# Second feed-forward: the rank-2 product of gate*up with a2, from one TensorE product a step to a VectorE sum a block

## The chip, the cores and the metric

One NeuronCore of a Trainium2 chip runs the whole kernel. The metric is the device time of one execution in microseconds (us), the median of several runs; lower is better. Engines: TensorE (PE; PEld is its weight load), VectorE (DVE), ScalarE (ACT), GpSimd (POOL), SyncE (SP, which issues DMAs).

## The reference, cut to what matters

```python
x = layernorm(x + attn(x, w_gate, w_up, w_down))            # first feed-forward, sparse, 2752 wide
def qlora(x, wq, A, B):
    w = jnp.tile(wq, (1, 4))                                # wq holds a quarter of the input columns
    return x @ w.T + (x @ A.T @ B.T) * 0.5                  # A, B of rank 2
gate = silu(qlora(x, w1q, a1, b1)); up = qlora(x, w3q, a3, b3)
x = layernorm(x + qlora(gate * up, w2q, a2, b2))            # second feed-forward
```

x has 2048 tokens of 1024 values, all in float32; the hidden width is 2752. Because w2 is tiled four times, the product of gate*up (called h) with it needs only the sum of h over its four quarters, 688 wide. The rank-2 product h @ a2.T needs all 2752 values of h.

## The kernel before

Tokens go in four blocks of 512 (NB, TB). The first feed-forward fills most of the time; the change concerns the second, which starts near 1690 us and is written in functions named with _2. Every float32 operand of a product is split into a high part (type fp32r) and a low part, the remainder; ScalarE makes the high part, GpSimd the low one (`low`, line 465), and TensorE adds three products (`three`, lines 1277 to 1279).

A block has 22 steps (STEPS), m = 4c + q. c is one of six chunks of the quarter's 688 rows (five of 128, the last of 112 for a pair of quarters), q the quarter; the last chunk has two steps. In a step TensorE makes gate and up of 128 hidden rows by 512 tokens: six 512-column products and one low-rank product (line 1448) for each, in PSUM banks 2(m%2) and 2(m%2)+1. ScalarE takes silu of the gate into sg (line 831), VectorE multiplies with up into h2 (line 1197) and adds h2 to fold (lines 1205, 1208) for q over 0. ScalarE splits h2 into h2h (line 817), GpSimd makes h2l (line 570), and TensorE multiplies both with a2s, the split a2 of that step, into bank 4 (`low_h`, lines 1420 and 1423), two steps behind. When a chunk's fold is complete ScalarE makes hqh (line 822) and GpSimd hql (line 576).

After the steps, `down_2` multiplies hqh and hql with w2 for four token tiles (t) and two halves (n), and adds the low-rank part t2s x b2s (line 1478). Between tiles the next block's x1 is transposed (line 1401), copied (line 807), multiplied with a1 and a3 (line 1410) and summed over quarters by VectorE (`fold_x`, lines 1166 to 1172). VectorE's `low_rank_h` takes bank 4 into t2s (lines 1223 to 1226).

The order of work is written by hand: each engine runs its instructions in program order and waits on semaphores. What matters here:
- TensorE's gate of step m waits until ScalarE has read the bank of step m-2, its up until VectorE has (h_done).
- A chunk's first step waits for the low parts (w13l) of its four weight pieces. The pieces of chunk c+1 are loaded when chunk c-1 has been used (pe_used), made high by ScalarE in steps q of chunk c, and low by GpSimd in the same steps, in its queue before that step's other work.
- In steps 1 to 4 VectorE also takes the mean and variance of the previous block's y (lines 1067 to 1072); GpSimd's `inv_std` (line 507) waits for it in its queue at step 5.
- The last c of down_2's first half waits for all six hql.

Of the kernel before, what the change touches and what calls it, by code (L numbers as in the profile page):

```python
# [26 lines left out]
P = 128  # L27
# [37 lines left out]
NW2, NW13 = 2 * CQ, 4 * CQ  # L65
USED2 = USED0 + USEDB * (NB - 1) + ND
# [50 lines left out]
def program(nc, xT, xtok, wg, wu, wd, w13, w2, a13, a2, b1, b3, b2, out):  # L117
    x1 = nc.dram_tensor("x1", (NB, P, NT, H), F32, kind="Internal").ap()
    with ExitStack() as ctx:
        def sem(name):  # L120
            return ctx.enter_context(nc.semaphore(name))
# [83 lines left out]
        a2s = put("a2s", [P, STEPS, 2 * R], F32R)  # L205
# [3 lines left out]
        t2s = put("t2s", [P, TB], F32R)  # L209
        assert over["at"] <= at["hTh"]  # L210
# [18 lines left out]
        h2 = put("h2", [P, 2, TB], F32)  # L229
        h2h = put("h2h", [P, 2, TB], F32R)  # L230
        h2l = put("h2l", [P, 2, TB], F32R)
# [9 lines left out]
        def down_done_with(name, h):  # L241
# [4 lines left out]
        hql = put("hql", [P, CQ, TB], F32R)  # L246
        assert over["at"] <= at["junkd"]

# [18 lines left out]
        small_in, b_zero, b_in, b_ready, a_ready, keep_ready = (  # L267
            sem("small_in"), sem("b_zero"), sem("b_in"), sem("b_ready"), sem("a_ready"), sem("keep_ready"))
        l_fold = sem("l_fold")
        x1t_done, x1t_ready, t1_done, l_ready = sem("x1t_done"), sem("x1t_ready"), sem("t1_done"), sem("l_ready")  # L270
        gg_done, uu_done, s_done, h_done, f_done = (
            sem("gg_done"), sem("uu_done"), sem("s_done"), sem("h_done"), sem("f_done"))
        hh_done, hl_done, t2_done, t2_ready = sem("hh_done"), sem("hl_done"), sem("t2_done"), sem("t2_ready")
# [179 lines left out]
        def _(pool):  # L453
# [80 lines left out]
            for d in range(ND):  # L534
                sl = slice((d % 4) * 512, (d % 4 + 1) * 512)
                rows = rows_in(NC - 1 - d // 2)
                low(LAST_D + d, wh[0:rows, sl], wl[0:rows, sl], w_in_place[0:rows, sl])
                if d == 4:

                    pool.wait_ge(t_done, NC * NB)  # L540
                    nc.gpsimd.memset(keep[:], 1.0).then_inc(pool_s, 1)
                    pool.wait_ge(pool_s, 3)
                    nc.gpsimd.affine_select(out=keep[:, 0:1], in_=keep[:, 0:1], compare_op=ALU.is_ge, fill=0.0,
                                            base=R - 1, pattern=[[0, 1]], channel_multiplier=-1).then_inc(keep_ready, 1)
                    nc.gpsimd.affine_select(out=keep[:, 1:2], in_=keep[:, 1:2], compare_op=ALU.is_ge, fill=0.0,
                                            base=-R, pattern=[[0, 1]], channel_multiplier=1).then_inc(keep_ready, 1)
                    nc.gpsimd.memset(t2s[0:LR, :].bitcast(F32), 0.0).then_inc(keep_ready, 1)
                if d == 19:
# [16 lines left out]
            def steps_2(b, last):  # L565

                def low_h(m):
                    rows = place(m)[2]
                    pool.wait_ge(hh_done, STEPS * b + m + 1)
                    nc.gpsimd.tensor_tensor(h2l[0:rows, m % 2, :], h2[0:rows, m % 2, :],  # L570
                                            h2h[0:rows, m % 2, :].bitcast(F32), ALU.subtract).then_inc(hl_done, 1)
# [17 lines left out]
                low_h(STEPS - 1)  # L589
# [17 lines left out]
        def _(act):  # L607
# [202 lines left out]
            def steps_2(b, before):  # L810

                def high_h(m):
                    rows = place(m)[2]
                    act.wait_ge(h_done, STEPS * b + m + 1)
                    if m >= 2:
                        act.wait_ge(t2_done, STEPS * b + m - 1)
                    nc.scalar.copy(h2h[0:rows, m % 2, :], h2[0:rows, m % 2, :]).then_inc(hh_done, 1)  # L817

                def high_q(c):
                    rows = rows_of(c)  # L820
                    act.wait_ge(f_done, CQ * b + c + 1)
                    nc.scalar.copy(hqh[0:rows, c, :], fold[0:rows, :]).then_inc(qh_done, 1)

                for m in range(STEPS):
                    c, q, rows = place(m)
                    if c < CQ - 1:
                        high_13(b, c + 1, q)
                    act.wait_ge(gg_done, STEPS * b + m + 1)
# [3 lines left out]
                    if m:  # L832
                        high_h(m - 1)
                    if q == 0 and c:
                        high_q(c - 1)
# [8 lines left out]
                high_h(STEPS - 1)  # L844
# [28 lines left out]
        def _(dve):  # L873
# [261 lines left out]
            with dve.Fori(1, NB) as b:  # L1135
# [12 lines left out]
            step(V.tensor_copy(a2s[:, :, 0:R], a2raw[:, :, :]))  # L1148
            st.done()
            V.tensor_tensor(a2s[:, :, R:2 * R], a2raw[:, :, :], a2s[:, :, 0:R].bitcast(F32), ALU.subtract)\  # L1150
                .then_inc(a_ready, 1)
# [37 lines left out]
            def steps_2(b):  # L1189
                for m in range(STEPS):  # L1190
# [9 lines left out]
                    last = q == steps_of(c) - 1  # L1200
                    ins = None
                    if q == 1:
                        if c:
                            dve.wait_ge(ql_done, CQ * b + c)
                        ins = V.tensor_tensor(fold[0:rows, :], h2[0:rows, 0, :], h2[0:rows, 1, :], ALU.add)
                    elif q > 1:
                        st.done()
                        ins = V.tensor_tensor(fold[0:rows, :], fold[0:rows, :], h2[0:rows, m % 2, :], ALU.add)
                    if last:
                        ins.then_inc(f_done, 1)  # L1210
                        dve.wait_ge(f_done, CQ * b + c + 1)
                    elif ins is not None:
                        step(ins)
# [5 lines left out]
            def low_rank_h(b):  # L1219

                n = 2 * R
                dve.wait_ge(t2_done, STEPS * (b + 1))
                step(V.tensor_copy(t2s[0:n, :], banks[4][0:n, :]))
                step(V.tensor_copy(t2s[64:64 + n, :], banks[4][0:n, :]))
                st.done()
                V.tensor_tensor(t2s[32:32 + n, :], banks[4][0:n, :], t2s[0:n, :].bitcast(F32), ALU.subtract)\
                    .then_inc(t2_ready, 1)
# [44 lines left out]
        def _(pe):  # L1272
# [141 lines left out]
            def low_h(b, m, frees):  # L1414

                c, q, rows = place(m)
                pe.wait_ge(hl_done, STEPS * b + m + 1)
                pe.sem_inc(passed_pe, 1)
                w = a2s[0:rows, m, :]
                i1 = nc.tensor.matmul(banks[4][0:2 * R, :], w, h2h[0:rows, m % 2, :], start=m == 0, stop=False)  # L1420
                if frees:
                    i1.then_inc(pe_used, 4)
                nc.tensor.matmul(banks[4][0:2 * R, :], w, h2l[0:rows, m % 2, :], start=False,
                                 stop=m == STEPS - 1).then_inc(t2_done, 1)

            def steps_2(b):
# [3 lines left out]
                for m in range(STEPS):  # L1430
# [8 lines left out]
                    for i, (low_x, done) in enumerate(((lg, gg_done), (lu, uu_done))):  # L1439
# [4 lines left out]
                        for k in range(KQ):  # L1444
                            s, mm = (c % 2) * 4 + 2 * i + k, slice(q * rows, (q + 1) * rows)
                            three(dst, w13h[:, s, mm], w13l[:, s, mm], xsh[:, k, :], xsl[:, k, :], k == 0, False)
                        mm = slice(c * Q4 * P + q * rows, c * Q4 * P + (q + 1) * rows)
                        nc.tensor.matmul(dst, b13[0:LR, mm], low_x[0:LR, :], start=False, stop=True).then_inc(done, 1)  # L1448
                    if m >= 2:
                        low_h(b, m - 2, q == steps_of(c) - 1)  # L1450
                low_h(b, STEPS - 2, False)

            def down_2(b, t, between=None):
# [8 lines left out]
                for n in range(2):  # L1462
                    w = slice(n * 512, (n + 1) * 512)
                    for c in range(CQ):
                        rows = rows_of(c)
                        if t == n == 0 and c == CQ - 1:
                            low_h(b, STEPS - 1, False)
# [19 lines left out]
            pe.wait_ge(a_ready, 1)  # L1487
# [78 lines left out]
```

## Time and profile before

| | |
|---|---|
| median of 3 runs | 2202.78 us (2202.04 to 2204.5) |
| profiled execution, span from first to last instruction | 2205.2 us (no other time of this execution is given) |
| TensorE busy | 2058.3 us, 93% |
| VectorE busy | 1110.3 us, 50% |
| GpSimd busy | 1053.4 us, 48% |
| ScalarE busy | 782.8 us, 35% |

The profile records one execution. Busy times of TensorE overlap in part, as matmuls are pipelined. A row of the timeline has the start in us, the duration in us, engine, line, operation, output and inputs, and in brackets the idle time before it and what released it.

### The profile page before, as it was taken

What the parts mean: (1) busy time and instruction counts of PE and PEld (TensorE: products, weight loads), DVE (VectorE), ACT (ScalarE), POOL (GpSimd) and SP (SyncE); (2) the same over time, 40 slices, a digit from 0 to 9 for tenths busy, and PEclk for the clock granted to TensorE, in tenths of its full rate; (3) what the DMA queues carried; (4) which work ended last, traced back from release to release, by engine and by line L of the source; (5) the groups of instructions that cost most, each with busy time, mean ns of one, the idle gap of its engine ahead of it and who ended that gap; (6) DMA issues with size and microseconds to landing.
All of it is one profiled execution on the core that took longest, in us unless ns stands there. A gap on an engine that the chain in (4) does not pass through costs nothing.

```text
span 2205.2 us, 32819 instructions
## 1 busy us (share of the span) xinstructions
PE 2058.3 (93%) x11008; PEld 1834.4 (83%) x11008; DVE 1110.3 (50%) x1794; ACT 782.8 (35%) x1280; POOL 1053.4 (48%) x744
## 2 busy tenths in 40 slices
PE   8998949999799899979989999799997999999998
PEld 8997939978699898869989888798786777777776
DVE  0145863368665234886533479654005444453543
ACT  3345323354133234612333363132233515334151
POOL 6444734435344443444454345343474827447281
PEclk9998969999899998989999999898999999999999
DMA  4332403322343332233433223244332412314030
GB/s 128 96 92 63 127 15 91 88 82 96 111 124 114 92 91 72 96 121 90 121 111 92 73 96 130 78 122 131 121 108 78 143 57 86 133 38 151 32 138 39
DMA packets 90356, 213.47 MB, mean 97 GB/s; under 512 B 10360, under 2 KB 12408, under 8 KB 89188
## 3 DMA queue, kind: packets, MB, share of 16 engines
q1 hardware_dynamic: 85616, 194.97, 28.8%
q10 hardware_dynamic: 4608, 16.78, 2.0%
q8 instruction: 78, 1.28, 0.2%
q14 instruction: 54, 0.44, 0.1%
HBM read 194.93 MB, written 16.78 MB: 96 GB/s over the span
## 4 chain that ended last, share of the span: by engine, by line
PE 71%; issue 11%; POOL 8%; DVE 5%; ACT 3%; DMA 2%; SPq 0%; POOLq 0%; ACTq 0%; DVEq 0%
PE bank L1277 22%; PE bank L1278 22%; PE bank L1279 22%; POOL wl L465 3%; POOL h2l L570 2%; ACT junka L672 2%; POOL w13l L465 2%; PE bank L1410 1%; DVE v L1122 1%; PE bank L1448 1%; DMA w_in_place<-in_wu 1%; PE bank L1309 1%; DMA w_in_place<-in_wd 1%; DVE scr L969 1%; ACT wh L613 1%
## 5 line engine op out<-in xcount | busy, mean ns | idle before, releaser
L465 POOL TENSOR_TENSOR wl<-w_in_place,wh 128x688 fp32r<-128x688 f32 (+1 forms) x432 | 680.1, 1576 | 826.5 <-ACT wh L613 806.1
L1277 PE MATMUL bank<-wh,xTh 128*128 128x344 f32 x2048 | 666.9, 326 | 79.4 <-POOL wl L465 49.5
L1279 PE MATMUL bank<-wh,xTl 128*128 128x344 f32 x2048 | 662.5, 323 | 0.0
L1278 PE MATMUL bank<-wl,xTh 128*128 128x344 f32 x2048 | 661.6, 323 | 0.0
L613 ACT CAST wh<-w_in_place 128x688 fp32r<-128x688 f32 (+1 forms) x432 | 305.3, 707 | 929.1 <-DMA w_in_place<-in_wu 352.8
L1277 PEld LDWEIGHTS bank<-wh,xTh 128*128 128x128 f32 x2048 | 392.0, 191 | 83.2 <-issue 68.7
L1278 PEld LDWEIGHTS bank<-wl,xTh 128*128 128x128 f32 x2048 | 392.4, 192 | 0.0
L1279 PEld LDWEIGHTS bank<-wh,xTl 128*128 128x128 f32 x2048 | 391.6, 191 | 0.0
L1277 PE MATMUL bank<-wh,hTh 128*128 128x512 f32 (+1 forms) x704 | 284.6, 404 | 11.8 <-ACT v L642 6.6
L1278 PE MATMUL bank<-wl,hTh 128*128 128x512 f32 (+1 forms) x704 | 283.1, 402 | 0.0
L1279 PE MATMUL bank<-wh,hTl 128*128 128x512 f32 (+1 forms) x704 | 282.6, 401 | 0.0
L465 POOL TENSOR_TENSOR w13l<-w_in_place,w13h 128x512 fp32r<-128x512 f32 (+1 forms) x96 | 124.6, 1303 | 187.1 <-ACT w13h L613 186.9
L1277 PEld LDWEIGHTS bank<-wh,hTh 128*128 128x128 f32 (+1 forms) x704 | 137.3, 195 | 46.9 <-issue 13.6
L905 DVE TENSOR_SCALAR sgn<-v x96 | 69.5, 724 | 204.4 <-ACT v L642 204.4
L672 ACT ACTIVATE junka<-v,negt 128x1376 int8<-128x1376 f32 x96 | 138.3, 1441 | 76.0 <-DVE negt L915 76.0
L1279 PEld LDWEIGHTS bank<-wh,hTl 128*128 128x128 f32 (+1 forms) x704 | 137.5, 195 | 29.8
L1278 PEld LDWEIGHTS bank<-wl,hTh 128*128 128x128 f32 (+1 forms) x704 | 137.5, 195 | 28.8
L1277 PE MATMUL bank<-xsh,w13h 128*128 128x512 f32 (+1 forms) x352 | 140.6, 399 | 9.0 <-DVEq L1187 5.5
L921 DVE TENSOR_SCALAR_CACHE_REDUCE junkd<-v,tc 128x2752 int8<-128x2752 f32 x48 | 147.6, 3076 | 0.9
L1197 DVE TENSOR_TENSOR h<-bank,sg 128x512 f32<-128x512 f32 (+1 forms) x88 | 60.8, 691 | 171.6 <-PE bank L1448 153.7
L1113 DVE TENSOR_TENSOR hTl<-bank,hTh 128x512 fp32r<-128x512 f32 x88 | 55.6, 683 | 180.6 <-ACT hTh L690 180.4
L570 POOL TENSOR_TENSOR h2l<-h,h2h 128x512 fp32r<-128x512 f32 (+1 forms) x88 | 120.2, 1366 | 44.2 <-ACT h2h L817 44.2
(128 smaller groups left out, 2535.9 us busy)
## 6 DMA issues: line engine op xcount, KB each, us to landing
w_in_place<-in_wg SPq DMA_DIRECT2D x128, 344.0 KB, 2.9
w_in_place<-in_wu SPq DMA_DIRECT2D x128, 344.0 KB, 2.9
w_in_place<-in_wd SPq DMA_DIRECT2D x168, 256.0 KB, 2.6
w_in_place<-in_w SPq DMA_DIRECT2D x90, 256.0 KB, 3.7
x_in_place<-in_xT SPq DMA_DIRECT2D x32, 256.0 KB, 3.4
y<-in_xtok SPq DMA_DIRECT2D x4, 2048.0 KB, 8.7
x<-y ACTq DMA_DIRECT2D x16, 512.0 KB, 3.5
xa<-x SPq DMA_DIRECT2D x16, 512.0 KB, 4.5
```

Of the source, the lines that this page charges most:

```text
L465: nc.gpsimd.tensor_tensor(lo, landed, hi.bitcast(F32), ALU.subtract).then_inc(done, 1)
L570: nc.gpsimd.tensor_tensor(h2l[0:rows, m % 2, :], h2[0:rows, m % 2, :], h2h[0:rows, m % 2, :].bitcast(F32), ALU.subtract).then_inc(hl_done, 1)
L613: nc.scalar.copy(hi, piece).then_inc(hi_done, 1)
L672: ins = nc.scalar.activation(junka[:, :], v[:, t, h * (I // 2):(h + 1) * (I // 2)], ACT.Sign, bias=negt[:, t:t + 1], accum_out=ssum[:, t - ...
L905: step(V.tensor_scalar(sgn[:, t, bass.ds((2 * jj + q) * CW, CW)], s, 0.0, 2.0, ALU.is_ge, ALU.mult))
L921: step(V.tensor_scalar(junkd[:, :], v[:, t, :], tc[:, 0, t:t + 1], None, ALU.is_lt, ALU.add, accum_out=tc[:, 1, t:t + 1]))
L969: step(V.scalar_tensor_tensor(out=scr[:], in0=v[:, t, c * Q:(c + 1) * Q], scalar=hc[:, 0, t:t + 1], in1=v[:, t, c * Q:(c + 1) * Q], op0=AL ...
L1113: V.tensor_tensor(hTl[0:rows, c, :], banks[4 * (j % 2) + m][0:rows, :], hTh[0:rows, c, :].bitcast(F32), ALU.subtract).then_inc(t_lo, 1)
L1197: V.tensor_tensor(h2[0:rows, m % 2, :], banks[2 * (m % 2) + 1][0:rows, :], sg[0:rows, m % 2, :], ALU.mult).then_inc(h_done, 1)
L1277: nc.tensor.matmul(dst, ah, bh, start=start, stop=False)
L1278: nc.tensor.matmul(dst, ah, bl, start=False, stop=False)
L1279: return nc.tensor.matmul(dst, al, bh, start=False, stop=stop)
```

## The change

The product of h with a2 is no longer made on TensorE in each step. VectorE keeps acc, two sums of 128 x 512 for each block, and adds h2 times a column of a2 to each in every step. After the last step it splits acc into acch and accl, and four products with sel (ones in one column for each rank row) add them over partitions, into bank 4, within down_2 of tile 0 (n = 1, before c = 3). The sum over quarters moves from VectorE to GpSimd (`fold_h`). h2h and h2l are gone, h2 has four buffers instead of two, and the weights' buffers are released at the last product of a chunk's up. t2s is filled by two operations instead of three, behind which fold_x of the next block's first tile stands in VectorE's queue. hqh is made at q = 1 of the next chunk instead of q = 0.

```diff
 VectorE, steps_2
-                    if m >= 2:
-                        dve.wait_ge(hl_done, STEPS * b + m - 1)
+                    if m >= H2N:
+                        dve.wait_ge(folded, FOLDS * b + folds_by(m - H2N))
...
-                        ins = V.tensor_tensor(fold[0:rows, :], h2[0:rows, 0, :], h2[0:rows, 1, :], ALU.add)
...
+                    for r in range(R):
+                        w, total = a2raw[0:rows, m, r:r + 1], acc[0:rows, r, :]
+                        if m == 0:
+                            step(V.tensor_scalar(total, hm, w, None, ALU.mult))
+                        else:
+                            step(V.scalar_tensor_tensor(out=total, in0=hm, scalar=w, in1=total, op0=ALU.mult, op1=ALU.add))
 VectorE, low_rank_h
+                step(V.tensor_copy(acch[:, :, :], acc[:, :, :]))
+                st.done()
+                V.tensor_tensor(accl[:, :, :], acc[:, :, :], acch[:, :, :].bitcast(F32), ALU.subtract).then_inc(acc_ready, 1)
+                dve.wait_ge(t2_done, b + 1)
+                step(V.tensor_copy(t2s[0:LR, :], banks[4][0:LR, :]))
+                st.done()
+                V.tensor_tensor(t2s[32:64, :], banks[4][32:64, :], t2s[32:64, :].bitcast(F32), ALU.subtract)\
 GpSimd, steps_2
+                def fold_h(m):
+                    c, q, rows = place(m)
+                    pool.wait_ge(h_done, STEPS * b + m + 1)
+                    if q > 1:
+                        pool.wait_ge(folded, FOLDS * b + m - c - 1)
+                    elif c:
+                        pool.wait_ge(ql_done, CQ * b + c)
+                    before = h2[0:rows, (m - 1) % H2N, :] if q == 1 else fold[0:rows, :]
+                    nc.gpsimd.tensor_tensor(fold[0:rows, :], before, h2[0:rows, m % H2N, :], ALU.add).then_inc(folded, 1)
...
-                    if m:
-                        low_h(m - 1)
-                    if q == 0 and c:
+                    if q == 1 and c:
                         low_q(c - 1)
+                    if m and q != 1:
+                        fold_h(m - 1)
                     if m == 5:
                         inv_std(NB + b - 1)
 TensorE
-            def low_h(b, m, frees):
-                pe.wait_ge(hl_done, STEPS * b + m + 1)
...
+            def low_h(b):
+                pe.wait_ge(acc_ready, b + 1)
+                for r in range(R):
+                    nc.tensor.matmul(banks[4][0:LR, :], sel[:, r, :], acch[:, r, :], start=r == 0, stop=False)
+                    ins = nc.tensor.matmul(banks[4][0:LR, :], sel[:, r, :], accl[:, r, :], start=False, stop=r == R - 1)
+                ins.then_inc(t2_done, 1)
```

## Rows read from the trace of the kernel before

**Rows 1.** The page's first part: busy us, share of the span, instructions.
```profile
PE 2058.3 (93%) x11008; PEld 1834.4 (83%) x11008; DVE 1110.3 (50%) x1794; ACT 782.8 (35%) x1280; POOL 1053.4 (48%) x744
```

**Rows 2.** Busy time by stretch: PE, PEld, DVE, ACT, POOL, granted clock, DMA.
```profile
1818.47:1901.40 82.93, 81.58 (x350) 61.01 (x351) 39.29 (x54) 40.31 (x73) 59.40 (x47) 1.00 0.35 120
```

**Rows 3.** Timeline of TensorE, the first matmuls of two steps.
```profile
1828.69 0.40 PE L1277 MATMUL bank<-xsh,w13h 128*128 128x512 f32 x1
...
1832.39 0.40 PE L1277 MATMUL bank<-xsh,w13h 128*128 128x512 f32 x1
```

**Rows 4.** Timeline of VectorE in steps 1 and 7 of the second block.
```profile
1825.20 0.69 DVE L1197 TENSOR_TENSOR h<-bank,sg 128x512 f32<-128x512 f32 x1 [2.41 <-PE bank L1448]
1825.93 0.69 DVE L1205 TENSOR_TENSOR fold<-h 128x512 f32<-128x512 f32 x1
1826.54 1.28 DVE L1067 BATCH_NORM_STATS2 stats<-y 128x6 f32<-128x512 f32 x2
1827.97 0.21 DVE L1069 BATCH_NORM_AGGREGATE mv<-stats 128x2 f32<-128x12 f32 x1 [0.15 <-DVE stats L1067]
...
1847.74 1.78 DVE L1208 TENSOR_TENSOR fold<-fold,h 128x512 f32<-128x512 f32 x1
```

**Rows 5.** Timeline of GpSimd in the same block.
```profile
1826.03 1.75 POOL L465 TENSOR_TENSOR w13l<-w_in_place,w13h 128x512 fp32r<-128x512 f32 x1
...
1842.52 1.01 POOL L507 TENSOR_TENSOR rstd<-ve,mhalf 128x4 f32<-128x4 f32 x1
...
1847.70 1.27 POOL L570 TENSOR_TENSOR h2l<-h,h2h 128x512 fp32r<-128x512 f32 x1
...
1867.85 1.29 POOL L570 TENSOR_TENSOR h2l<-h,h2h 128x512 fp32r<-128x512 f32 x1
1869.10 1.28 POOL L576 TENSOR_TENSOR hql<-fold,hqh 128x512 fp32r<-128x512 f32 x1
```

**Rows 6.** Two lines with durations min/median/max in ns; one group with its mean.
```profile
L1085 DVE SCALAR_TENSOR_TENSOR v<-v,tc x96: 565/577/2074, 590.6 to 1513.1; 128x344 f32<-128x344 f32 x96
...
L969 DVE SCALAR_TENSOR_TENSOR scr<-v,hc x32: 1650/1654/2707, 229.4 to 1369.5; 128x1376 f32<-128x1376 f32 x32
...
L1184 DVE TENSOR_SCALAR lg<-th,keep 4x512 fp32r<-4x512 f32 x6 | 2.9, 476 | 0.2
```

**Rows 7.** Timeline of VectorE and GpSimd near 290 us, merged rows.
```profile
289.16 5.55 DVE L1122 SCALAR_TENSOR_TENSOR v<-v,tc,w 128x344 f32<-128x344 f32 x4
...
289.70 2.77 POOL L465 TENSOR_TENSOR xTl<-x_in_place,xTh 128x512 fp32r<-128x512 f32 x2 [6.94 <-ACT xTh L628]
```

**Rows 8.** Timeline of ScalarE and TensorE: refill of chunk 2, start of step 8.
```profile
1835.08 0.62 ACT L613 CAST w13h<-w_in_place 128x512 fp32r<-128x512 f32 x1 [3.47 <-DMA w_in_place<-in_w]
...
1848.13 0.47 PE L1277 MATMUL bank<-xsh,w13h 128*128 128x512 f32 x1 [0.78 <-POOL w13l L465]
```

**Rows 9.** Timeline of TensorE after an idle time, and the stretch behind it.
```profile
1599.67 0.79 PE L1277 MATMUL bank<-wh,hTh 128*128 128x512 f32 x1 [3.26 <-POOL wl L465]
...
1600.00:1606.00 6.00, 6.00 (x15) 4.65 (x15) 0.00 (x0) 1.24 (x2) 2.33 (x3) 0.51 0.34 133
```

**Rows 10.** Timelines of TensorE and VectorE at the end of the steps.
```profile
1899.52 0.39 PE L1448 MATMUL bank<-lu,b 96*112 96x512 f32 x1
...
1900.95 0.39 PE L1420 MATMUL bank<-h2h,a2s 112*4 112x512 f32 x1 [0.58 <-POOL h2l L570]
...
1905.72 0.40 PE L1420 MATMUL bank<-h2h,a2s 112*4 112x512 f32 x1
...
1899.94 0.69 DVE L1197 TENSOR_TENSOR h<-bank,sg 112x512 f32<-112x512 f32 x1 [3.00 <-PE bank L1448]
```

**Rows 11.** Timeline of VectorE in the down matmuls of tile 0 and 1.
```profile
1906.39 0.68 DVE L1223 CAST t2s<-bank 4x512 fp32r<-4x512 f32 x1 [5.03 <-PE bank L1423]
...
1908.53 1.98 DVE L1166 TENSOR_REDUCE xf<-x1T 128x256 f32<-128x1024 f32 x1
...
1917.87 1.10 DVE L1170 CAST xsh<-xf 128x256 fp32r<-128x256 f32 x1
```

More of the change, by code:

```diff
@@ L65 @@
 NW2, NW13 = 2 * CQ, 4 * CQ
+H2N = 4
+FOLDS = STEPS - CQ
 USED2 = USED0 + USEDB * (NB - 1) + ND
@@ L78, in steps_of, with folds_to, folds_by @@
     return Q4 if c < CQ - 1 else Q4 // 2
+def folds_to(c):
+    return (Q4 - 1) * (c + 1) if c < CQ - 1 else FOLDS
+def folds_by(m):
+    c, q, _ = place(m)
+    done = m + 1 if q == 0 else m
+    return done - place(done)[0]
 def place(m):
@@ L209, in program @@
         t2s = put("t2s", [P, TB], F32R)
+        sel = put("sel", [P, R, LR], F32R)
         assert over["at"] <= at["hTh"]
@@ L228, in program @@
         sg = put("sg", [P, 2, TB], F32)
-        h2 = put("h2", [P, 2, TB], F32)
-        h2h = put("h2h", [P, 2, TB], F32R)
-        h2l = put("h2l", [P, 2, TB], F32R)
+        h2 = put("h2", [P, H2N, TB], F32)
         fold = put("fold", [P, TB], F32)
@@ L246, in program @@
         hql = put("hql", [P, CQ, TB], F32R)
+        acch = put("acch", [P, R, TB], F32R)
+        accl = put("accl", [P, R, TB], F32R)
         assert over["at"] <= at["junkd"]
+        acc = sb("acc", [P, R, TB], F32, 4, offset=at["scr"])
         banks = [bank(f"bank{i}") for i in range(8)]
@@ L547, in _ @@
                     nc.gpsimd.memset(t2s[0:LR, :].bitcast(F32), 0.0).then_inc(keep_ready, 1)
+                    nc.gpsimd.memset(sel[:, :, :].bitcast(F32), 0.0).then_inc(pool_s, 1)
+                    pool.wait_ge(pool_s, 4)
+                    for r in range(R):
+                        nc.gpsimd.memset(sel[:, r, :].bitcast(F32).rearrange("p (g k) -> p g k", g=3)[:, :, r:r + 1],
+                                         1.0).then_inc(sel_ready, 1)
                 if d == 19:
@@ L827, in steps_2 @@
                         high_13(b, c + 1, q)
+                    if q == 1 and c:
+                        high_q(c - 1)
                     act.wait_ge(gg_done, STEPS * b + m + 1)
@@ L1147, in _ @@
             dve.wait_ge(small_in, 16 * 2)
[L1148 to L1151, printed above, removed]
             dve.wait_ge(b_ready, 2)
@@ L1193, in steps_2 @@
                     dve.wait_ge(s_done, STEPS * b + m + 1)
-                    if m >= 2:
-                        dve.wait_ge(hl_done, STEPS * b + m - 1)
+                    if m >= H2N:
+                        dve.wait_ge(folded, FOLDS * b + folds_by(m - H2N))
                     st.done()
-                    V.tensor_tensor(h2[0:rows, m % 2, :], banks[2 * (m % 2) + 1][0:rows, :], sg[0:rows, m % 2, :],
-                                    ALU.mult).then_inc(h_done, 1)
+                    hm = h2[0:rows, m % H2N, :]
+                    V.tensor_tensor(hm, banks[2 * (m % 2) + 1][0:rows, :], sg[0:rows, m % 2, :], ALU.mult).then_inc(h_done, 1)
                     dve.wait_ge(h_done, STEPS * b + m + 1)
[L1200 to L1204, printed above, removed]
-                        ins = V.tensor_tensor(fold[0:rows, :], h2[0:rows, 0, :], h2[0:rows, 1, :], ALU.add)
[L1206 to L1213, printed above, removed]
+                    for r in range(R):
[4 more added lines that the diff above has]
+                            step(V.scalar_tensor_tensor(out=total, in0=hm, scalar=w, in1=total, op0=ALU.mult, op1=ALU.add))
                     if 1 <= m <= NT:
@@ L1412, in low_rank @@
                 ins.then_inc(t1_done, 1)
-            def low_h(b, m, frees):
-                c, q, rows = place(m)
-                pe.wait_ge(hl_done, STEPS * b + m + 1)
+            def low_h(b):
+                pe.wait_ge(acc_ready, b + 1)
                 pe.sem_inc(passed_pe, 1)
[L1419 to L1424, printed above, removed]
+                for r in range(R):
+                    nc.tensor.matmul(banks[4][0:LR, :], sel[:, r, :], acch[:, r, :], start=r == 0, stop=False)
+                    ins = nc.tensor.matmul(banks[4][0:LR, :], sel[:, r, :], accl[:, r, :], start=False, stop=r == R - 1)
+                ins.then_inc(t2_done, 1)
             def steps_2(b):
@@ L1445, in steps_2 @@
                             s, mm = (c % 2) * 4 + 2 * i + k, slice(q * rows, (q + 1) * rows)
-                            three(dst, w13h[:, s, mm], w13l[:, s, mm], xsh[:, k, :], xsl[:, k, :], k == 0, False)
+                            ins = three(dst, w13h[:, s, mm], w13l[:, s, mm], xsh[:, k, :], xsl[:, k, :], k == 0, False)
+                        if i == 1 and q == steps_of(c) - 1:
+                            ins.then_inc(pe_used, 4)
                         mm = slice(c * Q4 * P + q * rows, c * Q4 * P + (q + 1) * rows)
                         nc.tensor.matmul(dst, b13[0:LR, mm], low_x[0:LR, :], start=False, stop=True).then_inc(done, 1)
-                    if m >= 2:
-                        low_h(b, m - 2, q == steps_of(c) - 1)
-                low_h(b, STEPS - 2, False)
             def down_2(b, t, between=None):
@@ L1465, in down_2 @@
                         rows = rows_of(c)
+                        if t == 0 and n == 1 and c == 3:
+                            low_h(b)
                         if t == n == 0 and c == CQ - 1:
-                            low_h(b, STEPS - 1, False)
                             pe.wait_ge(ql_done, CQ * (b + 1))
@@ L1486, in _ @@
             pe.wait_ge(b_ready, 4)
[L1487 removed]
+            pe.wait_ge(sel_ready, R)
             pe.wait_ge(keep_ready, 5)
```

35 lines of the change are left out of this document (7 added, 28 removed).

## The prediction

> **What bounds the kernel now.** I read the page's engine shares first. TensorE is busy 93% of the span; an average that says nothing of the second feed-forward [rows 1]. So I cut that out by stretches: each of its four blocks has 22 steps and then its down matmuls, and the steps of the second block take 82.93 us with 350 matmuls [rows 2]. Then the TensorE timeline: a step of sixteen 512-column matmuls runs from 1828.69 to 1832.39, 3.70 us, or 0.231 a matmul; the recorded 0.40 overlaps [rows 3]. 350 x 0.231 is 80.9 of the 82.93; two waits, 0.78 for w13l and 0.58 for h2l, make most of the rest [rows 8, 10]. So the steps are bound by TensorE today, with almost nothing under it to spare.
>
> But the work around it is near that bound. GpSimd is busy 59.4 and VectorE 39.3 of the 82.93 [rows 2], and the timelines of both show that they exclude each other. GpSimd's h2l starts at 1847.70, VectorE's fold at 1847.74 and takes 1.78 instead of 0.69: it is held 1.09. The other way round, the fold of 1825.93 makes w13l take 1.75 instead of 1.29 [rows 4, 5]. h = bank x sg, with one input in PSUM, takes 0.69 beside anything [rows 10]. GpSimd operations follow each other at 1.25 when nothing is in the way [rows 5]. With a fold of 0.69 between two of them, the fold of 1825.93 ends at 1826.62 and w13l at 1827.78, so one operation takes 1.16 after its release; the held fold ends 0.55 after h2l, not 0.69. The two overlap by 0.14, and one GpSimd operation plus one fold cost about 1.70, of which 1.01 is GpSimd's.
>
> **The change, part by part (block time T from 1818.47, us).**
>
> *TensorE.* Each block loses 22 x 2 matmuls and gains 4: 40 x 0.231 = 9.2, 37.0 over four blocks, if TensorE stays the bound. A step becomes 14 x 0.231 = 3.23.
>
> *VectorE.* One fold in 16 of 22 steps goes; two accumulations a step come. The trace has no 512-wide scalar_tensor_tensor with two SBUF inputs and a column scalar, but it has 344 wide at 0.577 and 1376 wide at 1.654 (the medians) [rows 6]: 1.04 ns an element, 0.75 for 512. Bounds: the 0.69 of a fold, and 0.75 plus a held 1.09. The first step's two tensor_scalar are 0.48, by the 4x512 form [rows 6].
>
> *GpSimd.* 22 h2l go and 16 folds come, 48 full or half operations become 42. All of them read SBUF.
>
> *The shared access.* Two accumulations in a row do not keep GpSimd out. In the first phase four such instructions (0.57 each) took 5.55 between 289.16 and 294.71, with GpSimd's xTl in between [rows 7]: they alternate, 2.28 of work and 3.27 of waiting. So in a steady step with two GpSimd operations (w13l and a fold or hql) the cycle is 2 x (1.01 + 0.75), 3.5 to 3.6 with the gaps, above TensorE's 3.23 and just below today's 3.70. This is the middle of the sum. Bounds: 3.23 (never in the way) and 2 x 1.25 + 1.5 = 4.0 (nothing overlaps).
> The Trainium skill says under "SBUF — State Buffer", Who interferes with whom, that a VectorE instruction with two SBUF inputs contends with a GpSimd instruction that reads SBUF and that the loser waits for the whole instruction. That speaks against this change. Taken literally with the 1.29 of the rows it makes a pair 2.04, a step 4.1 and four such steps 16.3 where the rows' overlap gives 14.3; I go by the rows, which overlap.
>
> *Steps 0 to 7.* VectorE also does the previous block's statistics in steps 1 to 4: bn_stats from 1826.54 to bn_aggr's end 1828.18, 1.64 [rows 4]. Such a step costs it 0.73 (h) + 1.5 + 1.0 (a GpSimd fold wedged in, released by the same h) + 1.67 (the statistics and a gap) = 4.9 against a 3.23 step. h(1) can start at T 6.7, as now (1825.20 less 1818.47 is 6.73) [rows 4]. Then h(2) 11.6, h(3) 16.5, h(4) 21.6, and h(5) 25.7 (no fold wedged in, plus ve). TensorE reuses a bank after two steps: up of step 6 (due at 21.0) waits for h(4) until 22.35, 1.35; up of step 7 then waits 0.85 for h(5) and ends at 28.0. GpSimd's queue is w13l(2,1), hql, then inv_std (1.01 [rows 5]), which waits for ve at 25.7; queued behind it are w13l(2,2), the fold of h(5) and w13l(2,3), for which step 8's matmuls wait. 26.7 + three operations of 1.25 + three accumulations in their way (0.5 each; 1.75 against 1.29 is 0.46 for a fold) = 32.0. Today step 8 starts at 1848.13, T 29.7 [rows 8]. TensorE idles 28.0 to 32.0.
> The refill is no later than now: its loads wait for the last matmuls of a chunk, and w13h of the first piece starts at 1835.08, T 16.6 [rows 8].
>
> *The clock.* After an idle of 3.26 TensorE ran 15 matmuls 0.43 apart, at a granted clock of 0.50, the 1.2 GHz level, in 1600 to 1606 [rows 9]. A 4.0 idle I take to do the same: 15 x 0.20 = 3.0 lost. Ends: 0 and 3.0.
>
> *Steps 8 to 21.* The first chunk of four takes TensorE 12.9 + 3.0 = 15.9 and the two other engines 14.3 (8 GpSimd operations of 1.01, 8 accumulations of 0.75, gaps): 15.9. The next takes 14.3 less 0.9, what the two engines can use of their lead: 13.4. The chunk after it has half-size pieces and takes TensorE's 12.9, the last two steps 6.5. Together 48.7: the stretch ends at 80.7 (82.93 now). Ends: 29.7 + 14 x 3.23 = 74.9, and 36 + 51 = 87.
>
> *Down stretch.* Today h(21) starts 0.42 after the last up matmul (1899.52, 1899.94), and TensorE gets to the last c of the down matmuls at 1905.72 without a wait [rows 10]. Afterwards it gets there after eight transposes and 15 matmuls, 3.46; the transposes are 1905.72 - 3.46 less 1901.41 (1900.95 + 2 x 0.231), 0.85, together 4.3 after the steps; the chain it needs is 0.2 + h 0.69 + accumulation 0.75 + fold 1.15 on GpSimd + hqh 0.6 + cast of acc + hql 1.15 + gaps 0.3. The cast (0.48 for 512 wide, so 0.5 to 1.0 for 1024; I take 0.8) stands in GpSimd's way, since a 256 wide one of 1917.87 was held to 1.10 itself [rows 6, 11]: 5.6. Wait 1.3 (0 to 2.5). Two matmuls more, 0.46. The t2s chain (two operations of 0.68 [rows 11] after 0.43) takes 1.8 and ten matmuls 2.3 lie before its use: hidden, 0.4 to spare. fold_x(t=0) moves behind it, some 5 us later. The low-rank matmuls of tile 1 want its x1T 5.0 after tile 0 ends (0.85 + 18 x 0.231); fold_x's reduce takes 2.0 [rows 11], two copies and gaps as much again: hidden, 1.0 to spare.
> The setup (a2s gone, memsets of sel on GpSimd in the last down phase) I cost at nothing: twelve matmuls a piece, 2.8, lie over a w piece of 1.25. Without that cover it is 1 us once.
>
> **Sum.** Per block 80.7 + 1.3 + 0.46 against 82.93 is -0.5; four blocks about -2: 2203.2 by the profiled execution, whose span of 2205.2 lies 2.4 above the median of the runs, so 2201 as a median. The matmuls saved are spent on two engines that shut each other out.
>
> **Rivals.**
> *TensorE stays near the bound (faster).* If VectorE does both accumulations before GpSimd gets in, steps 1 to 4 cost 3.9 each, step 8 starts at about 29.3, no idle is long enough for the clock and the middle chunks take 13.6: 29.3 + 27.2 + 12.9 + 6.5 + 1.8 = 77.7, -5.3 a block, 2182. For it: a fold that starts within 0.14 of the end of h2l isn't held. Against it: [rows 7], where they alternate.
> *The statistics and inv_std hold the queue (slower).* If in steps 1 to 4 both accumulations wait for a whole GpSimd operation (w13l and a fold), VectorE loses 1.0 more a step, inv_std comes 4 later, step 8 at 36 and TensorE idles 8 in a row. +4 a block: 16 - 2, 2217. It decides from 1.6 a block on, which takes the whole 4.4 above now. For it: folds held for 1.09 today. Against: GpSimd has one operation only in steps 0 and 1, and waits for h itself in 2 and 3.
> *It doesn't do what it says (no collision, full gain)*: -37 + 4 x 1.8 = -30, 2173; against it are the held pairs of [rows 4, 5], and I give it a small part of the faster case.
>
> **How the numbers follow.** 0.2%, 4.4 us, is about what a measurement of this kernel can tell from no change. Forecast case 0.45, its own range 2195 to 2207: 0.10 faster, 0.28 same, 0.07 slower. Faster rivals 0.33, slower rival 0.22. Together 0.43, 0.28, 0.29. The range runs from the middle of the fast rival to half way into the slow one, 2183 to 2213.
>
> **What would show it.** Right: 308 matmuls in a step stretch of 80 to 82; accumulations with a minimum of 0.75 and a mean over 1.1; folds on GpSimd over 1.5; TensorE waiting for w13l at step 8 by some 4 us in each block, a granted clock of 0.5 behind it; h(4) and h(5) late. Wrong: w13l waits under 1 us and a mean accumulation under 0.9 (the fast rival), or h late throughout and step 8 beyond T 34 (the slow one). If no wait for ql appears in the down stretch, that term was mis-sized.

## The result, and the profile after

| | median of runs | ratio to the runs of before, 95% |
|---|---|---|
| before | 2202.78 us (7 runs) | |
| changed | 2214.55 us (7 runs) | 1.0048 (1.0032 to 1.0063) |
| changed, second series | 2219.1 us (10 runs; before beside it 2206.39) | 1.0055 (1.0035 to 1.0076) |

The change makes the kernel 0.5% slower, 10.6 to 12 us, where 2201 had been forecast. The profiled execution has a span of 2209.3, only 4.1 above that of before; its run is the shortest of the seven (2211.05 with what lies around the span), while the span of before alone is above the median of its runs. So these two profiles show only part of the loss; the other part is seen in the further profiles below. Medians of different series are not to be subtracted: a series is compared by its ratio to the runs of before beside it.

The page's first part of the changed kernel, the same columns as [rows 1]: TensorE is busy 25 us less and VectorE 149 more.
```profile
PE 2032.8 (92%) x10848; PEld 1825.4 (83%) x10848; DVE 1259.6 (57%) x1908; ACT 738.9 (33%) x1192; POOL 1063.6 (48%) x723
```
The four step stretches by window, columns as [rows 2]; the second answers to it. 308 matmuls instead of 350, but 80.99 instead of 82.93, and in three of the four stretches a granted clock under 1.00 (before, 0.97 in the first stretch and 1.00 in the others):
```profile
1686.10:1771.05 84.95, 76.95 (x308) 60.74 (x309) 69.14 (x77) 29.42 (x50) 58.08 (x40) 0.94 0.33 117
1819.71:1900.70 80.99, 72.78 (x308) 57.27 (x309) 71.55 (x79) 29.42 (x50) 59.39 (x40) 1.00 0.35 123
1949.21:2031.87 82.66, 75.17 (x309) 59.11 (x310) 73.01 (x79) 29.64 (x50) 59.63 (x40) 0.96 0.35 120
2080.39:2163.75 83.36, 75.86 (x308) 59.61 (x309) 70.00 (x79) 29.43 (x50) 58.16 (x40) 0.96 0.27 94
```
Before, these stretches took 84.99, 82.93, 82.98 and 82.69. The saving is 0.0, 1.9, 0.3 and -0.7, 1.6 in all.

VectorE in steps 3 to 5 of the second block (it answers to [rows 4]; two accumulations are merged in a row), block time T counted from 1819.71:
```profile
1836.21 0.69 DVE L1209 TENSOR_TENSOR h<-bank,sg 128x512 f32<-128x512 f32 x1
1836.94 2.72 DVE L1216 SCALAR_TENSOR_TENSOR acc<-h,a2raw,acc 128x512 f32<-128x512 f32 x2
1839.59 1.27 DVE L1082 BATCH_NORM_STATS2 stats<-y 128x6 f32<-128x512 f32 x2
1841.01 0.21 DVE L1084 BATCH_NORM_AGGREGATE mv<-stats 128x2 f32<-128x12 f32 x1 [0.15 <-DVE stats L1082]
1841.38 0.69 DVE L1209 TENSOR_TENSOR h<-bank,sg 128x512 f32<-128x512 f32 x1 [0.16 <-DVE mv L1084]
1842.11 1.42 DVE L1216 SCALAR_TENSOR_TENSOR acc<-h,a2raw,acc 128x512 f32<-128x512 f32 x2
...
1845.39 0.69 DVE L1209 TENSOR_TENSOR h<-bank,sg 128x512 f32<-128x512 f32 x1
```
Two accumulations take 1.42 when GpSimd is idle (it waits for ve then) and 2.72 when it is not. GpSimd beside them (answers to [rows 5]):
```profile
1837.37 1.74 POOL L596 TENSOR_TENSOR fold<-fold,h 128x512 f32<-128x512 f32 x1
1839.08 1.74 POOL L480 TENSOR_TENSOR w13l<-w_in_place,w13h 128x512 fp32r<-128x512 f32 x1
1840.78 1.26 POOL L601 TENSOR_TENSOR hql<-fold,hqh 128x512 fp32r<-128x512 f32 x1
1845.37 1.02 POOL L522 TENSOR_TENSOR rstd<-ve,mhalf 128x4 f32<-128x4 f32 x1 [3.33 <-DVE ve L1087]
1846.36 1.66 POOL L480 TENSOR_TENSOR w13l<-w_in_place,w13h 128x512 fp32r<-128x512 f32 x1
1847.98 1.71 POOL L596 TENSOR_TENSOR fold<-h 128x512 f32<-128x512 f32 x1
1849.65 1.72 POOL L480 TENSOR_TENSOR w13l<-w_in_place,w13h 128x512 fp32r<-128x512 f32 x1
```
And TensorE's waits in that block, with what ended each: up of step 6, up of step 7, gate of steps 8, 12 and 16, and the down matmuls' wait for the last hql (answers to [rows 8, 10]):
```profile
1842.22 0.47 PE L1282 MATMUL bank<-xsh,w13h 128*128 128x512 f32 x1 [1.30 <-DVE h L1209]
...
1846.23 0.47 PE L1282 MATMUL bank<-xsh,w13h 128*128 128x512 f32 x1 [0.55 <-DVE h L1209]
...
1851.76 0.47 PE L1282 MATMUL bank<-xsh,w13h 128*128 128x512 f32 x1 [3.68 <-POOL w13l L480]
...
1866.43 0.47 PE L1282 MATMUL bank<-xsh,w13h 128*128 128x512 f32 x1 [1.29 <-POOL w13l L480]
...
1880.97 0.47 PE L1282 MATMUL bank<-xsh,w13h 128*128 128x512 f32 x1 [1.39 <-POOL w13l L480]
...
1905.56 0.47 PE L1282 MATMUL bank<-w2h,hqh 112*128 112x512 f32 x1 [0.39 <-POOL hql L601]
```
The stretches behind the wait at step 8 in the second and third block (answers to [rows 9]). Waits of 3.68 and 3.66 stand before them; behind the second the clock is at the 1.2 GHz level for part of the stretch, behind the first it is not:
```profile
1851.80:1857.00 5.20, 5.20 (x23) 4.19 (x24) 5.13 (x6) 1.06 (x2) 4.68 (x3) 1.00 0.21 78
...
1981.20:1987.20 6.00, 5.95 (x16) 4.72 (x17) 4.67 (x5) 1.82 (x3) 4.72 (x3) 0.57 0.13 49
```
What such a drop costs is seen in GpSimd's queue. Its first w13l for step 16, in the second block (no drop) and in the third (drop), waits for w13h:
```profile
1869.54 1.30 POOL L480 TENSOR_TENSOR w13l<-w_in_place,w13h 128x512 fp32r<-128x512 f32 x1 [1.80 <-ACT w13h L638]
...
2000.70 1.30 POOL L480 TENSOR_TENSOR w13l<-w_in_place,w13h 128x512 fp32r<-128x512 f32 x1 [3.11 <-ACT w13h L638]
```
In block time that is T 49.8 and 51.5. The loads of these pieces wait until TensorE has used the chunk of steps 8 to 11, and are issued at T 45.4 and 47.8. So a slower TensorE also sends the two other engines off later, and the third block is 1.7 longer.

The groups of the changed kernel's second feed-forward (behind the bar: busy us, mean ns of one): accumulations 1258 ns where 0.75 us is their own price, w13l and fold 1578 and 1631 ns instead of 1.29 us.
```profile
L1216 DVE SCALAR_TENSOR_TENSOR acc<-h,a2raw,acc 128x512 f32<-128x512 f32 x152 | 185.2, 1258 | 2.7
L480 POOL TENSOR_TENSOR w13l<-w_in_place,w13h 128x512 fp32r<-128x512 f32 x75 | 118.2, 1578 | 165.0 <-ACT w13h L638 165.0
L596 POOL TENSOR_TENSOR fold<-fold,h 128x512 f32<-128x512 f32 x40 | 65.2, 1631 | 18.1 <-DVE h L1209 18.1
```
Something else stands before the second feed-forward begins, near 1590. GpSimd waits 6.22 for TensorE before the memset of braw (the buffer of the low-rank weights), and TensorE then waits 4.60 and 1.64 for wl behind it (first GpSimd, then TensorE):
```profile
1586.86 3.27 POOL L570 MEMSET braw<- 96x3808 f32 x1 [6.22 <-PE bank L1284]
...
1591.40 0.80 PE L1282 MATMUL bank<-wh,hTh 128*128 128x512 f32 x1 [4.60 <-POOL wl L480]
...
1601.54 0.50 PE L1282 MATMUL bank<-wh,hTh 128*128 128x512 f32 x1 [1.64 <-POOL wl L480]
```
In the kernel before the memset waits for nothing, and one wait of 3.26 stands there [rows 9]:
```profile
1584.79 3.28 POOL L550 MEMSET braw<- 96x3808 f32 x1
```

### The profile page after: what moved, and what is told of

Read it like the earlier page. It is cut to its first block, busy times and chain, and to the rows that moved or that the text cites. A ratio compares the mean times of both kernels' runs of the same rounds, so it can differ in the third digit from the quotient of the medians.

```text
span 2209.3 us, 32337 instructions
## 1 busy us (share of the span) xinstructions
PE 2032.8 (92%) x10848; PEld 1825.4 (83%) x10848; DVE 1259.6 (57%) x1908; ACT 738.9 (33%) x1192; POOL 1063.6 (48%) x723
## 4 chain that ended last, share of the span: by engine, by line
PE 60%; issue 15%; POOL 9%; DVE 9%; ACT 3%; DMA 2%; POOLq 0%; DVEq 0%; SPq 0%; ACTq 0%
PE bank L1282 19%; PE bank L1284 19%; PE bank L1283 19%; POOL wl L480 5%; DVE acc L1216 3%; ACT junka L697 2%; POOL fold L596 2%; PE bank L1415 1%; DVE h L1209 1%; DVE v L1137 1%; DMA w_in_place<-in_wd 1%; POOL w13l L480 1%; POOL hql L601 1%; DVE stats L1082 1%; PE bank L1314 1%
## 5 line engine op out<-in xcount | busy, mean ns | idle before, releaser
L480 POOL TENSOR_TENSOR w13l<-w_in_place,w13h 128x512 fp32r<-128x512 f32 (+1 forms) x96 | 137.9, 1440 | 185.3 <-ACT w13h L638 185.3
L1216 DVE SCALAR_TENSOR_TENSOR acc<-h,a2raw,acc 128x512 f32<-128x512 f32 (+1 forms) x168 | 202.3, 1243 | 2.9
L1283 PE MATMUL bank<-xsl,w13h 128*128 128x512 f32 (+1 forms) x352 | 142.4, 405 | 0.0
```

What stands on the lines that cost most here:

```text
L480: nc.gpsimd.tensor_tensor(lo, landed, hi.bitcast(F32), ALU.subtract).then_inc(done, 1)
L1216: step(V.scalar_tensor_tensor(out=total, in0=hm, scalar=w, in1=total, op0=ALU.mult, op1=ALU.add))
L1283: nc.tensor.matmul(dst, ah, bl, start=False, stop=False)
```

## The experiments

Each profile is cut at the first step: what lies before it (A) and from there to the end (B). B is the second feed-forward; A repeats to a few us only, and B of the changed kernel to 3. Each other row is one profile.

| kernel | A | B | median | ratio to before, 95% |
|---|---|---|---|---|
| before, two profiles | 1686.1, 1682.5 | 519.1, 520.0 | 2202.78 | |
| changed, two profiles | 1686.1, 1697.5 | 523.2, 526.3 | 2214.55 | 1.0048 |
| acc in PSUM | 1688.7 | 484.6 | 2174.42 | 0.9868 (0.9849 to 0.9887) |
| one accumulation | 1696.0 | 492.9 | 2189.0 | 0.9927 (0.9909 to 0.9946) |
| none | 1691.8 | 483.5 | 2176.37 | 0.9873 (0.9852 to 0.9895) |
| statistics spread | 1690.9 | 519.4 | 2212.77 | 1.0047 (1.0029 to 1.0066) |
| layout as before | 1684.6 | 522.2 | 2208.63 | 1.0020 (1.0003 to 1.0036) |
| TensorE kept busy | 1691.8 | 514.8 | 2208.23 | 1.0007 (0.9992 to 1.0022) |
| inv_std later | 1689.2 | 522.6 | 2211.96 | 1.0044 (1.0027 to 1.0062) |
| PSUM, spread, layout | 1686.0 | 483.6 | 2171.31 | 0.985 (0.9828 to 0.9872) |
| PSUM, layout, inv_std later | 1687.1 | 482.2 | 2165.79 | 0.9824 (0.9798 to 0.9851) |

**Accumulators in PSUM.**
```diff
-                        w, total = a2raw[0:rows, m, r:r + 1], acc[0:rows, r, :]
+                        w, total = a2raw[0:rows, m, r:r + 1], banks[(4, 7)[r]][0:rows, :]
```
and acch, accl are taken from the banks, one r at a time; the next block's low-rank products into bank 7 wait for that.

> The changed kernel with acc kept in PSUM (banks 4 and 7) instead of SBUF, so an accumulation has one SBUF input; it is split into acch and accl from there. Theory A (the two engines shut each other out over SBUF): an accumulation takes about 0.75 us without being held (1.24 mean now), the folds and w13l on GpSimd go back to 1.3, a statistics step costs VectorE 3.95 instead of 4.9, TensorE waits for w13l at step 8 by 1.7 instead of 3.6, later chunks not at all; steps 74 to 75 us a block, the whole about 2175 to 2182. Theory B (VectorE simply has too much work in steps 1 to 4, whoever else reads SBUF): the waits at step 8 stay over 3 us and the time within 5 of the changed kernel, 2208 or more.

Measured 2174.42, 1.8% or 40 us under the changed kernel by the ratios, and 0.6 under the range of theory A. The number of instructions on VectorE and GpSimd is the same but for two more splits a block. The groups (same columns as above):
```profile
L1216 DVE SCALAR_TENSOR_TENSOR bank<-h,a2raw,bank 128x512 f32<-128x512 f32 x152 | 107.5, 753 | 2.7
L480 POOL TENSOR_TENSOR w13l<-w_in_place,w13h 128x512 fp32r<-128x512 f32 x75 | 96.6, 1291 | 183.0 <-ACT w13h L638 183.0
L596 POOL TENSOR_TENSOR fold<-fold,h 128x512 f32<-128x512 f32 x40 | 51.7, 1292 | 13.7 <-DVE h L1209 13.7
```
All three are back at their own price, the step stretch of the second block is 73.4, and TensorE waits for w13l only 1.24 at step 8. So it is not VectorE's amount of work that did the harm but where the accumulator lies. The edit moves both its reading and its writing out of SBUF. That the writing is harmless is seen in the changed kernel itself: h (bank x sg, one SBUF input, written to SBUF) takes 691 ns on average there and never over 694, while the accumulations beside it were held, and 692 here. What is left is the second SBUF input. The Trainium skill has the rule in "SBUF — State Buffer", Who interferes with whom: a VectorE instruction with at most one SBUF input, outside the two-port modes, does not contend with GpSimd. The trace agrees, 753 against 1258 ns.

**One accumulation a step, and none.**
```diff
-                    for r in range(R):
+                    for r in range(R if m == 0 else 1):      # none: else 0
```
Both kernels leave out part of the low-rank sum; they serve to measure its cost.

> The changed kernel with one accumulation a step instead of two (the second rank row gets the first step alone: part of the low-rank sum is left out). Theory A: a step then has 2 x 1.01 + 0.75 of shared access, 2.8, below TensorE's 3.23, so the waits of steps 12 and 16 vanish and that of step 8 shrinks to under 1.5: 2182 to 2190. Theory B: the statistics steps cost VectorE 3.2 to 4.2, the wait at step 8 shrinks likewise, but later chunks, where VectorE has room, should not change.

> The changed kernel with no accumulation after the first step (nearly all of the low-rank sum is left out). It measures the whole cost of VectorE's part: with TensorE's 40 matmuls a block gone and nothing in the way, both theories expect steps of 71 to 72 us a block and a down stretch 0.5 to 1 longer, 2168 to 2175. If it stays above 2190, something else of the change costs (fold on GpSimd, the order of the queues).

2189.0 is as A expected; 2176.37 is 1.4 above its range, as the steps took 71.9 to 73.9 a block instead of 71 to 72, and the down stretches 1.4 to 2.4 more than before instead of 0.5 to 1. With one, B is 492.9; with none 483.5, and with both in PSUM 484.6: in PSUM the accumulations cost 1 us, in SBUF the first costs 9 and the second another 30 to 33. The wait of step 12 went with one accumulation, but the expectation failed for the others: step 16 still waited 0.65 to 1.65, and step 8 waited 1.6 to 2.0, not under 1.5.

**The statistics spread out.** Steps 1, 3, 5, 7; inv_std and bias in step 9, and ScalarE's normalisation two steps later (not shown).
```diff
-                    if 1 <= m <= NT:
-                        norm_sums(NB + b - 1, [m - 1])
+                    if m in (1, 3, 5, 7):
+                        norm_sums(NB + b - 1, [m // 2])
```


> The changed kernel with the previous block's statistics in steps 1, 3, 5, 7 instead of 1 to 4, inv_std and the bias in step 9 and the normalisation two steps later. Theory A and B both expect h(4) and h(5) in time and no long wait at step 8, and with it no drop of the clock there. A expects the saturated chunks to remain (steps 12 and 16 wait 1.3 to 2 for w13l, and now step 8 about as much): a gain of 2 to 3 a block, 2203 to 2207. B expects all waits gone: 2185 or less.

2212.77, a miss for both theories: the ratio is that of the changed kernel, though B of its one profile, 519.4, is 4 to 7 shorter. The wait at step 8 fell to 1.8 and came back at step 12 (second block, TensorE):
```profile
1851.52 0.47 PE L1282 MATMUL bank<-xsh,w13h 128*128 128x512 f32 x1 [1.86 <-POOL w13l L480]
...
1861.45 0.47 PE L1282 MATMUL bank<-xsh,w13h 128*128 128x512 f32 x1 [1.50 <-DVE h L1209]
...
1870.79 0.47 PE L1282 MATMUL bank<-xsh,w13h 128*128 128x512 f32 x1 [4.25 <-POOL w13l L480]
```
**inv_std later in GpSimd's queue.** In step 7, behind the last w13l of the chunk.
```diff
+                    if m == 7:
+                        inv_std(NB + b - 1)
                     if q == 1 and c:
                         low_q(c - 1)
...
-                    if m == 5:
-                        inv_std(NB + b - 1)
```


> The changed kernel with inv_std moved in GpSimd's queue from step 5 to step 7, behind the last w13l of that chunk. Theory E (at step 8 it is the place of inv_std, waiting for VectorE's statistics, that holds w13l): w13l(2,2) no longer waits 3.3 for ve plus 1.0 for the operation; what is left is h(5), at T 25.7, its fold and w13l(2,3), some 29.5: the wait of 3.6 at step 8 falls to about 1.5, too short for the clock, the waits for h stay; 2 to 3.5 a block, 2202 to 2208. If only the shared access sets it, the wait stays above 3.

The wait at step 8 fell to 1.3 to 1.6 as expected, but the time stayed: 2211.96 instead of 2202 to 2208. What it gave up came back: up of step 7 waited 1.5 instead of 0.5, and step 12 waited 3.5 instead of 1.3:
```profile
1853.01 0.47 PE L1282 MATMUL bank<-xsh,w13h 128*128 128x512 f32 x1 [1.60 <-POOL w13l L480]
...
1869.63 0.77 PE L1282 MATMUL bank<-xsh,w13h 128*128 128x512 f32 x1 [3.49 <-POOL w13l L480]
```
Both moves say the same. In the second block step 12 starts at T 46.7 in the changed kernel, 47.2 with the statistics spread and 47.6 with inv_std later: the two engines together owe about the same amount by step 12, and the order only chooses where TensorE waits for it.

**TensorE kept busy through the wait.**
```diff
+                    if m == 8:
+                        for k in range(12):
+                            nc.tensor.matmul(banks[4][0:LR, :], sel[:, 0, :], xsh[:, 0, :], start=True, stop=True)
```


> The changed kernel with twelve extra products (2.8 us, sel times xsh into bank 4, result unused) before TensorE's wait for w13l at step 8 in each block. They fit in the 3.6 wait. Theory D (the idle time also costs by the lower clock behind it): no stretch at a granted clock of 0.5 behind step 8, 1.0 to 1.7 us less a block where it dropped, 2 to 6 less in all. If the clock costs nothing beside the wait, the time is that of the changed kernel within 2.

2208.23, with 48 useless products more; beside it the changed kernel took 2219.1 (1.0007 against 1.0055). B is 514.8 against 523.2 and 526.3: 8 to 11, where I had expected 2 to 6. Behind step 8 of the second block, first the changed kernel's second profile, then this one:
```profile
1864.90:1870.90 6.00, 5.94 (x15) 4.72 (x16) 4.70 (x5) 1.79 (x3) 4.74 (x3) 0.55 0.16 62
```
```profile
1855.50:1861.50 6.00, 5.97 (x26) 4.95 (x27) 5.89 (x7) 1.79 (x3) 4.74 (x3) 1.00 0.20 72
```
No step stretch of this kernel shows a lowered clock after the first 7 us of B. In the two profiles of the changed kernel the clock records of the steps behind those first 7 us hold 20 and 31 us at the 1.2 GHz level; at half speed that is up to 10 and 15 of matmul time, against a gain of 8.4 and 11.5. By this kernel the drops of the clock make up the whole of the second feed-forward's loss: without them B is 4 to 5 below that of before, though the engines are as much in each other's way as in the changed kernel.

**The layout as it was.**
```diff
         fold = put("fold", [P, TB], F32)
+        pad = put("pad", [P, 2, TB], F32)
```
The change drops h2h and h2l, four buffers of 2 KB a partition, and gives h2 two more, so all that lies behind h2 moved down by 4 KB; pad puts lu, w13l and braw back.

> The changed kernel with two unused buffers of 2 KB a partition behind fold, so that lu, w13l and braw lie where they lay before the change. Theory C (part of the loss is the layout: without h2h and h2l the braw buffer moved down over a later-read part of hTl, so its memset waits for two more down pieces and holds wl): the wait of 4.6 goes, the memset runs without an idle wait as before, the start of the second feed-forward comes 2.5 to 4 earlier, the whole is 2 to 4 below the changed kernel. If the setup memsets of sel were the cause instead, nothing changes.

2208.63, and 2219.1 for the changed kernel beside it; the ratios differ by 0.35%, 7.7 us. The memset again runs without a wait before it, and TensorE's wait is 3.23 as in the kernel before, not 4.61 and 2.91 (first GpSimd, then TensorE):
```profile
1584.50 3.28 POOL L571 MEMSET braw<- 96x3808 f32 x1
...
1599.39 0.79 PE L1283 MATMUL bank<-wh,hTh 128*128 128x512 f32 x1 [3.23 <-POOL wl L481]
```
The memset's wait is computed from where braw lies over hTl; two buffers of 2 KB fewer put it two chunks of hTl lower, which are four down pieces (the expectation said two). The memsets of sel are still there in this kernel, so they are not the cause. Over all profiles, A is 1691.5 on average in eight with the changed layout (1686.1 to 1697.5) and 1685.2 in five with the old one (1682.5 to 1687.1): 6 us, twice what I had expected.

A few us of A are the first feed-forward's own spread, and the profiles can be cut once more to leave it out. Its last down phase starts at 1530.9 on average with the changed layout and at 1530.7 with the old one. From there to the first step it is 159.0 to 163.0 us (160.6 on average) in the eight and 152.7 to 156.3 (154.5) in the five. So the 6 us arise there, and no profile of one group lies in the range of the other. TensorE's waits for wl behind the memset are 6.8 on average against 3.1, so 3.7 of the 6. From 1580 to the first step the clock records hold 9.6 us at the 1.2 GHz level against 5.1; at half speed that is, by my estimate, the other 2.3.

**The changed kernel and the kernel before once more.**

> The changed kernel as it is, once more, beside the next three, for a second profile and more runs. The median should be again 8 to 12 above the kernel before. In the profile: step stretches of 81 to 83.5 us, a wait of 3.6 for w13l at step 8 of each block, and in the last down phase of the first feed-forward a wait of 4.6 for wl behind the memset of braw (6.2 us of idle GpSimd before it), none of which the kernel before has.

> The kernel before, for a second profile: which part of the difference between the two profiles shown first is the first feed-forward's own spread. Expected: 519 from the first step to the end as in the first profile (2205.2 - 1686.1), and a start of the steps anywhere from 1680 to 1690.

The median came 12.7 above that of before, where 8 to 12 had been expected, and the waits at the memset are as expected. The step stretches are 86.7, 84.4, 80.5 and 83.1, three of them outside 81 to 83.5, and in the third block step 8 waited 2.90, not 3.6. The first part took 11 us more than in the first profile; 7 of them lie before the last down phase. The kernel before gave 1.0011 (0.9993 to 1.0028) against itself, with a first step at 1682.5 and 520.0 behind it, as expected.

**Put together.**

> acc in PSUM, statistics in steps 1, 3, 5, 7 with inv_std in step 9, and the two unused buffers: what the first four runs point to. Theory A: without contention the wait of 1.25 at step 8 in the PSUM version comes from inv_std's place in GpSimd's queue and goes (4 x 1.2), the layout gives 3: 2163 to 2168.

> acc in PSUM, the two unused buffers, the statistics where the change has them, and inv_std behind the last w13l of its chunk (step 7). In the PSUM versions the chunk with inv_std in the middle waited 1.2; behind the w13l the operation falls in the time in which GpSimd waits for the next load. Expected: no wait for w13l above 0.4 in any chunk, 4 to 5 below the best so far: 2165 to 2168.

2171.31 misses its range: with inv_std in step 9 the wait moved from step 8 to step 12, 1.2 to 1.6. The last one, with inv_std behind the chunk's last w13l, gives 2165.79, in its range and 1.8% faster than before (0.9824, 0.9798 to 0.9851). That it beats the one before it is not shown: the intervals overlap, and B differs by 1.4. Waits of at most 0.4 had been expected; its waits for w13l in the second block, steps 8 and 16:
```profile
1836.61 0.47 PE L1286 MATMUL bank<-xsh,w13h 128*128 128x512 f32 x1 [0.69 <-POOL w13l L481]
...
1863.19 0.47 PE L1286 MATMUL bank<-xsh,w13h 128*128 128x512 f32 x1 [0.54 <-POOL w13l L481]
```
## Why the prediction was wrong, step by step

- *TensorE's matmuls (-37)*: right; the steps hold 308, and with no accumulation in the way ("none") B falls by 36. There the steps fall by 43, some 5 of which are waits that the kernel before had, and the down stretches rise by 7.
- *VectorE's accumulation, 0.75*: 0.737 at the least in SBUF, 0.753 on average in PSUM. Right.
- *Shared access, 3.5 to 3.6 a step*: right in kind and size. A GpSimd operation beside an accumulation takes 1.74 (1.76 by the sum), steps 8 to 16 take 14.6 a chunk (1851.76, 1866.43, 1880.97) instead of 14.3.
- *Steps 0 to 7*: right. Waits of 1.35, 0.85 and 4.0 were forecast, 1.30, 0.55 and 3.68 measured; step 8 at T 32.0 was forecast, and 1851.76 - 1819.71 is 32.05. (For h(4), 16.5 and 4.9 make 21.4, not 21.6; it came at 21.7.) inv_std waited 3.33 for ve in the place named.
- *Steps 8 to 21 and the clock*: this step failed by its size. The sum let a drop cost TensorE 3.0 but gave the two other engines a lead of it, which they were to use up in the next chunk: of the 3.0 only 0.7 a block was left (80.7 instead of 80.0), 2.8 over four blocks. They got no such lead. TensorE at half speed frees the chunk's buffers later, and GpSimd starts the next w13l 1.7 later. The wait of 1.29 at step 12 was covered by the drop, but step 16 waited 1.99 instead of 1.39, and the block took 82.66 instead of 80.99. A second drop, behind step 16's wait, was not in the sum; the first and fourth block had one. With useless products in the wait and so without drops, the four stretches add up to 322.7, just the forecast's 4 x 80.7; with the drops they are 332.0 and 334.7. So the drops cost 9 to 12 where the sum had 2.8. That the stretches without them meet the forecast is in part luck, since the forecast includes a drop. 1.6 was saved in all (nothing in the second pair of profiles), where 9 had been forecast.
- *Down stretch (+1.76 a block)*: right but for some 1 us. 48.66, 48.51 and 48.5 against 47.4, 47.4 and 47.2, and 2.1 more in the last: 5.7 in all for 7.0. The wait for hql, forecast as 1.3, is 0.4 to 0.5, and 1.32 in the last block, which has no transposes to cover it. TensorE has no wait for t2s or fold_x.
- *The setup at nothing*: this step failed. I counted the memsets of sel and asked what covers them; I did not ask what else the diff moves. Removing h2h and h2l moves the buffers behind them in that overlay, and `down_done_with` turns an address into a wait. It costs 6 us where the sum had 0, half of the whole loss, and takes place 100 us before the second feed-forward's first step, at an instruction that the diff does not touch.

The sum by the runs: 6 for the layout and 4 to 6 for the second feed-forward, against the forecast 0 and -2. From 2201 to 2214.55 is 13.6; the layout makes 6 of it and the steps 7 to 9, and the down stretches take 1 back. The slower rival's 2217 lies nearer to the result than the forecast, but by luck: it rested on both accumulations held for a whole GpSimd operation in steps 1 to 4 (3.5 a pair, where 2.72 was measured), step 8 at T 36 and an idle time of 8, and none of these happened.

## What to carry to other kernels

- Before moving work to VectorE beside a busy GpSimd, count for each instruction how many inputs it reads from SBUF. Keeping an accumulator in PSUM brought the cost of the same 176 instructions from 40 us or more down to 1. A cast needs a look of its own (last section).
- When a diff drops or adds a buffer in an overlay, list what is addressed behind it and which waits are computed from addresses. They can be far from the changed code.
- Where two engines are saturated together, moving a piece of their work only moved the wait. And a wait of 2 to 4 us on TensorE is to be priced with the clock behind it. The other engines gain no lead by it when TensorE releases the buffers for their next inputs.

## What the runs showed of the hardware that I had not expected

- The length of an idle time did not tell whether the clock fell. Idle times of 3.6 to 3.7 had the 1.2 GHz level behind them in some blocks (0.57 behind 1981) and not in others (1.00 behind 1851). In the changed kernel's second profile, one of 2.79 in front of 1763 had 3.4 us of it behind, and so had one of only 1.75; ten us later one of 2.90 had none. In the kernel with one accumulation a wait of 2.0 had none either. From the second profile, two timeline rows of TensorE, each with the stretch behind it (columns as [rows 2]):
```profile
1988.71 0.47 PE L1282 MATMUL bank<-xsh,w13h 128*128 128x512 f32 x1 [1.75 <-DVE h L1209]
...
1989.80:1993.20 3.40, 3.40 (x10) 2.62 (x9) 3.08 (x7) 0.00 (x0) 1.35 (x2) 0.50 0.00 0
...
1998.25 0.47 PE L1282 MATMUL bank<-xsh,w13h 128*128 128x512 f32 x1 [2.90 <-POOL w13l L480]
...
1998.30:2003.00 4.70, 4.70 (x21) 3.86 (x22) 4.63 (x6) 0.94 (x2) 4.66 (x3) 1.00 0.31 111
```
- Twelve useless products in front of a wait made the kernel faster (2208.23 against 2219.1 in the same series).
- A 1024-wide cast from SBUF to SBUF has one SBUF input only, and yet it and GpSimd shut each other out. It took 0.69 in the kernel with no accumulations, where it began just before a GpSimd fold, which then took 1.79; in the changed kernel it began behind hql and took 1.64 to 1.67.
